# Sixteen steps of a GRU recurrence written as one loop on PE, with one buffer for the state's fp16 parts

## What is computed

```python
def cell(h, x):
    gi = x @ W_ih + b_ih
    gh = h @ W_hh + b_hh
    i_r, i_z, i_n = jnp.split(gi, 3, axis=-1)
    h_r, h_z, h_n = jnp.split(gh, 3, axis=-1)
    r = jax.nn.sigmoid(i_r + h_r)
    z = jax.nn.sigmoid(i_z + h_z)
    n = jnp.tanh(i_n + r * h_n)
    h_new = (1.0 - z) * n + z * h
    return (h_new, h_new)
xs = jnp.swapaxes(inputs, 0, 1)
_, hs = jax.lax.scan(cell, initial_state, xs)
return jnp.swapaxes(hs, 0, 1)
```

## Time and profile before

| | us |
|---|---|
| median of three runs | 2298.03 |
| the three runs | 2296.30 to 2299.89 |
| the profiled execution | 2292.36 |
| span of the profiled execution | 2290.5 |
| PE busy | 2179.2 (95%) |
| DVE busy | 1528.3 (67%) |
| ACT busy | 1279.5 (56%) |

### The profile page before, as it was taken

How to read it: one execution, slowest core, us unless ns; L and a number is a source line. 1 busy time by engine, 2 the same in 40 slices (tenths; PEclk the granted TensorE clock), 3 DMA queues, 4 the chain that set the end, 5 groups by cost and what they waited for, 6 DMA issues and landing times.

```text
span 2290.5 us, 130384 instructions
## 1 busy us (share of the span) xinstructions
PE 2179.2 (95%) x56333; PEld 1837.8 (80%) x56333; DVE 1528.3 (67%) x6093; ACT 1279.5 (56%) x5574; POOL 485.6 (21%) x2271
## 2 busy tenths in 40 slices
PE   5768999999989999999999999999999999999998
PEld 3654655645545899999999999999999999999997
DVE  7987867768677456655665565566666566666665
ACT  6765947749468355566444454454545444454444
POOL 2002121021110122232222222222222222222222
PEclk8569999999999999999999999999999999999999
DMA  5000000010010000000000000000000000000000
GB/s 204 3 2 1 1 1 1 1 56 1 1 56 1 22 4 5 5 5 5 5 5 9 5 9 4 9 10 5 9 9 5 9 5 10 10 5 14 12 9 16
DMA packets 8711, 31.49 MB, mean 14 GB/s; under 512 B 1028, under 2 KB 1352, under 8 KB 7880
## 3 DMA queue, kind: packets, MB, share of 16 engines
q1 hardware_dynamic: 7712, 23.07, 2.7%
q10 hardware_dynamic: 424, 0.07, 0.0%
HBM read 18.94 MB, written 4.19 MB: 10 GB/s over the span
## 4 chain that ended last, share of the span: by engine, by line
PE 82%; DVE 11%; ACT 3%; issue 2%; DMA 1%; POOL 0%; SPq 0%; DVEq 0%; POOLq 0%; ACTq 0%
PE psum L1923 53%; PE psum L1830 9%; PE psum L1733 4%; PE psum L1654 3%; PE psum L1751 3%; PE psum L1696 2%; PE psum L1717 2%; PE psum L1857 2%; DVE region_cols L1102 2%; DVE region_cols L1086 2%; DVE top L1279 1%; PE psum L1673 1%; DMA region_cols<-in_L_cond_W_emb_dram 1%; PE psum L1766 1%; PE psum L1870 1%
## 5 line engine op out<-in xcount | busy, mean ns | idle before, releaser
L563 POOL TENSOR_TENSOR region_w_b<-region_w_b 128x16 f32<-128x16 f32 x1022 | 223.2, 218 | 1153.1 <-DVE region_w_b L1488 1153.1
L1923 PE MATMUL psum<-parts1A,region_w_hh 128*128 128x40 f16 x12288 | 429.6, 179 | 2.9 <-issue 1.1
L1923 PE MATMUL psum<-parts0A,region_w_hh 128*128 128x40 f16 x12288 | 428.9, 179 | 3.1 <-ACT psum L819 0.9
L1923 PE MATMUL psum<-parts1B,region_w_hh 128*128 128x40 f16 x12288 | 428.9, 179 | 1.1 <-issue 0.5
L1923 PE MATMUL psum<-parts0B,region_w_hh 128*128 128x40 f16 x12288 | 428.4, 179 | 1.1 <-issue 0.9
L1923 PEld LDWEIGHTS psum<-parts1A,region_w_hh 128*128 128x128 f16 x12288 | 381.1, 96 | 41.0 <-DVE parts1A L1497 5.7
L1923 PEld LDWEIGHTS psum<-parts0A,region_w_hh 128*128 128x128 f16 x12288 | 380.9, 96 | 40.2 <-DVE parts0A L1497 4.4
L915 ACT ACTIVATE mixA<-rzA 128x8 f32<-128x8 f32 x512 | 110.8, 216 | 535.1 <-DVE rzA L1462 535.1
L1923 PEld LDWEIGHTS psum<-parts1B,region_w_hh 128*128 128x128 f16 x12288 | 363.3, 96 | 3.3 <-issue 1.6
L1923 PEld LDWEIGHTS psum<-parts0B,region_w_hh 128*128 128x128 f16 x12288 | 362.9, 95 | 3.0 <-issue 1.5
L1462 DVE TENSOR_REDUCE rzA<-psum 128x8 f32<-128x32 f32 x512 | 98.2, 192 | 278.9 <-PE psum L1923 278.4
(11 more groups left out here) (243 smaller groups left out, 3303.1 us busy)
## 6 DMA issues: line engine op xcount, KB each, us to landing
region_rows<-in_x_dram SPq DMA_DIRECT2D x4, 1024.0 KB, 11.2
region_w_a<-in_L_cond_W_qkv_dram SPq DMA_DIRECT2D x1, 3072.0 KB, 23.2
region_w_hh<-in_L_cond_W_hh_dram SPq DMA_DIRECT2D x4, 768.0 KB, 6.6
region_w_a<-in_L_cond_W_ih_dram SPq DMA_DIRECT2D x1, 3072.0 KB, 10.2
out_dram<-region_w_b SPq DMA_DIRECT2D x12, 256.0 KB, 2.3
region_cond<-in_cond_dram SPq DMA_DIRECT2D x2, 1024.0 KB, 7.8
region_cols<-in_L_cond_W_emb_dram SPq DMA_DIRECT2D x1, 2048.0 KB, 19.7
region_w_out<-in_L_cond_W_out_dram SPq DMA_DIRECT2D x1, 1024.0 KB, 21.5
```

What stands on the lines that cost most here:

```text
L563: e.tensor_tensor(k.line[half][:, :, :, 1:3], new.unsqueeze(3).broadcast_to([P, 2, B, 2]), k.signs.unsqueeze(1).unsqueeze(1).broadcast_to( ...
L1923: made = e.matmul(k.slots(bank)[:, :, ch, :, 0:2], k.w16[:, 2 * read + c, part, NC * "rzn".index(g) + 2 * half + ch], k.parts[now][read][: ...
```

## The change

Steps 112 to 127 on PE become a loop (`Fori`) of 16 turns over one written-out step, which starts at an instruction address that is a multiple of 256. Waits that count steps (lowA, lowB, putA, putB) are made against a register there. For one body to serve odd and even steps, the parts have one buffer for each half, in all 512 steps. So DVE may write parts A only when PE has read the last step's: unit ABn, the last that reads half A, counts up a new semaphore readA, and `dve_parts` waits for it. For half B nothing is added. The waits of PE on zsumA, nlineA, zsumB and nlineB are left out in all steps. `DVE_STEP` goes from 14 to 15, which moves DVE's cuts (63 instead of 58).

```diff
-DVE_STEP = 14
+DVE_STEP = 15
...
-        self.parts = [[small(f"parts{parity}{half}", 2, B, 2, dtype=FP16) for half in "AB"] for parity in range(2)]
+        self.parts = [small(f"parts{half}", 2, B, 2, dtype=FP16) for half in "AB"]
...
-def dve_parts(e, k, half, st, nxt):
+def dve_parts(e, k, st, half):
     s = k.sem
     h = "AB"[half]
     spread = k.spread[half].rearrange("p c b q -> p (c b) q")
     e.wait_ge(s[f"line{h}"], st + 1)
-    e.tensor_tensor(k.parts[nxt][half][:].rearrange("p c b q -> p (c b) q"), spread[:, :, STATE_AT:HIGH_AT + 1:HIGH_AT - STATE_AT],
+    if half == 0:
+        e.wait_ge(s["readA"], st + 1)
+    e.tensor_tensor(k.parts[half][:].rearrange("p c b q -> p (c b) q"), spread[:, :, STATE_AT:HIGH_AT + 1:HIGH_AT - STATE_AT],
                     spread[:, :, HIGH_AT:NONE_AT + 1:NONE_AT - HIGH_AT], ALU.subtract).then_inc(s[f"low{h}"], 1)
...
+LOOP = (112, 128)
...
-    for st in range(S):
+    for st in range(LOOP[0]):
+        pe_step(e, k, st)
+        pe_side(e, k, st)
+    e.addr_align(256, max_nops=4)
+    with e.Fori(LOOP[0], LOOP[1]) as st:
+        pe_step(e, k, st, st)
+    for st in range(LOOP[1], S):
+        pe_step(e, k, st)
+        pe_side(e, k, st)
...
+def pe_step(e, k, st, turn=None):
+    s = k.sem
+    for u in GRU_UNITS:
...
+        if u in ("AAr", "BAr"):
+            if turn is None and st == 0:
+                e.wait_ge(s["gru_first"], 18)
+                e.wait_ge(s["w_kept"], NC)
+                e.wait_ge(s["w_low"], NC)
             else:
-                pe_row_products(e, k, *args, products, number)
+                e.wait_ge(s[f"low{u[0]}"], st)
+        if u in ("AAr", "ABr"):
+            e.wait_ge(s[f"put{h}"], st + 1)
...
+        if LAST_OF[g, h] == u:
+            made.then_inc(s[f"{g}_products{h}"], 1)
+        elif u == "ABn":
+            made.then_inc(s["readA"], 1)
```

More of the change, by code:

```diff
@@ L82 @@
 r_productsA z_productsA n_productsA r_productsB z_productsB n_productsB
-rsumA zsumA nlineA rsigA giveA tanhA lineA lowA keptA putA
+rsumA zsumA nlineA rsigA giveA tanhA lineA lowA keptA readA putA
 rsumB zsumB nlineB rsigB giveB tanhB lineB lowB keptB putB
@@ L1426, in dve_gru @@
         first = k.state[:, 0, 2 * half:2 * half + 2]
-        e.tensor_copy(k.parts[0][half][:, :, :, 1], first).then_inc(done, 1)
+        e.tensor_copy(k.parts[half][:, :, :, 1], first).then_inc(done, 1)
         e.tensor_copy(k.line[half][:, :, :, 2], first).then_inc(done, 1)
@@ L1430, in dve_gru @@
         e.wait_ge(done, 11 + 4 * half)
-        e.tensor_tensor(k.parts[0][half][:, :, :, 0], first, k.parts[0][half][:, :, :, 1], ALU.subtract).then_inc(done, 1)
+        e.tensor_tensor(k.parts[half][:, :, :, 0], first, k.parts[half][:, :, :, 1], ALU.subtract).then_inc(done, 1)
     e.addr_align(DVE_BLOCK, max_nops=4)
     for st in range(S):
-        nxt = (st + 1) % 2
         dve_r_sum(e, k, st, 0)
@@ L1442, in dve_gru @@
         if st + 1 < S:
-            dve_parts(e, k, 0, st, nxt)
+            dve_parts(e, k, st, 0)
         dve_n_line(e, k, st, 1)
@@ L1446, in dve_gru @@
         if st + 1 < S:
-            dve_parts(e, k, 1, st, nxt)
+            dve_parts(e, k, st, 1)
         if st in PLACE_STEPS:
@@ L1893, in pe_gru @@
         pe_gate_products(e, k, 0, j, range(NC), j)
-    at = {u: i for i, u in enumerate(GRU_UNITS)}
-    final_unit = {(h, g): max((r + h + g for r in "AB"), key=at.get) for h in "AB" for g in "rzn"}
-    for st in range(S):
[L1897 to L1929, removed]
-                pe_gate_products(e, k, *args, products, number)
-            elif kind == "late":
-                pe_late_products(e, k, *args, products, number)
-            elif kind == "next":
-                pe_next_products(e, k, *args, products, number)
-            else:
-                pe_row_products(e, k, *args, products, number)
@@ L1939, in build, with pe_side @@
+def pe_side(e, k, st):
+    for (kind, *args), number, products in SIDE.get(st, ()):
+        if kind == "gates":
+            pe_gate_products(e, k, *args, products, number)
+        elif kind == "late":
+            pe_late_products(e, k, *args, products, number)
+        elif kind == "next":
+            pe_next_products(e, k, *args, products, number)
+        else:
+            pe_row_products(e, k, *args, products, number)
 def build(nc, *args):
```

10 lines of the change are left out of this document (added).

## The result

| | before | after |
|---|---|---|
| median of 20 runs each, the same chip | 2295.24 us | 2300.34 us |
| lowest to highest | 2291.04 to 2300.52 | 2297.26 to 2305.45 |
| profiled execution: span | 2290.5 us | 2297.6 us |
| TensorE steps 111 to 128, start to start | 51.73 us | 55.10 us |

The ratio is 1.0023, with a 95% interval of 1.0015 to 1.0031: the kernel became **5.1 us slower** (3.4 to 7.1), which is about the size that a measurement can tell from no change. The forecast was +2.7 us (2300.7 us), and the time lies inside the range. That it is within 0.4 us of the forecast is luck: the 2.7 were added to a median of three runs (2298.03), the median of twenty is 2.8 us lower, and the difference came out 2.4 us larger. The likeliest case was a change of less than 4.6 us; the centre of the measurement lies just beyond that bound.

A forecast was written before the change was run, and what follows sets the result against it. The prediction took PE as the bound in steps with side product and half B's loop through DVE and ACT in steps 112 to 127. 3.3 - 0.6 + 0 + 0 = +2.7 us gave 2300.7 us, range 2296.0 to 2305.5.

The forecast's parts named there:

- Where the loop's block stands: Ahead of step 112: a block begins 8 instructions before it, so the alignment jumps over the other 248.
- The entry wait: Before step 112: PE waits once, 3.2 to 3.3 us, for the block jumped to; 3.3 us taken.
- Stalls that go: Steps 112 to 128: the loop's 15 further turns fetch nothing, so 0.6 us of fetch stalls go.
- The turn itself: Loop turns: register waits and branch cost 0 to 1.8 us for 16 turns; 0 taken, by half A's room.
- half A's 0.13 us of room: Steps without side product: PE would be ready for half B at 1124.41 but stands still until 1124.55.
- The one buffer, the waits taken out and DVE's cuts: All 511 steps: the readA wait, removed PE waits and 63 DVE cuts stay hidden; 0 us.
- The block is fetched again each turn: Loop's branch back: 15 turns each pay about 2.8 us, 42 us in all, 2343 us; chance 0.10.
- register waits cost more than the room: Loop turns: every 0.1 us beyond half A's room costs 1.6 us; at 0.2 a turn 2303.9 us; chance 0.17.
- the jump finds its block: Loop entry: no wait there, or the loop's fetches were never late; -0.6 us, 2297.4 us; chance 0.14.
- The fetch that the jump might start anew: Loop entry: the jump starts a fetch anew, doubling the entry wait to a sum of +6 us; chance 0.06.
- The change relieves fetching elsewhere: Recurrence: half of 6.4 us of issue waits go and entry costs nothing, -3.8 us, 2294.2 us; chance 0.06.
- Only one block is ahead: PE's code fetch: the next block's packet starts only when the block before it already runs.

The follow-up runs named there:

- experiment 3: The kernel before with only the alignment to 256 ahead of step 112, two buffers and no loop: 2285.63 us, ratio 1.0017 to before.
- experiment 6: The changed kernel again, no edit, on another chip, against the kernel before there: 2294.55 us, ratio 1.0013.
- experiment 7: The changed kernel with its aligned loop from step 114 on (14 turns), against the kernel before: 2293.83 us, ratio 1.0008.
- experiment 2: The changed kernel with the loop but without the alignment ahead of it, against the kernel before: 2282.78 us, ratio 1.0003.
- experiment 1: The changed kernel without loop or alignment, all 512 steps written out, against the kernel before: 2282.25 us, ratio 1.0003.
- Experiment 5: The changed kernel with the loop from step 113 on (15 turns), not aligned, against the kernel before: 2291.29 us, ratio 1.0001.
- experiment 4: The changed kernel with the loop from step 113 on (15 turns), alignment kept, against the kernel before: 2284.34 us, ratio 1.0009.
- experiment 8: The kernel before again, no edit, for its profile alone: 2289.72 us, one run.

## Why the prediction was right, and where it was wrong

**Where the loop's block stands**: right. The jump was at slot 8 of its block, and nearly the whole next fetch was still to come.

**The entry wait**, 3.3 us taken: 3.13 us in the first profile, 2.90 in experiment 3, 3.58 in experiment 6. The sum was right for the wrong parts. The packet started 0.65 us after the side product, not the 1.39 of the earlier trace rows (0.50 in experiment 3, 1.44 in experiment 6); it took 1.28 us, not 0.96; and the first load came 1.72 us after it had landed, not 1.4 to 1.5. The last number is firm: 1.7 in experiments 3 and 6 too. It is the 1.4 to 1.5 of the earlier trace rows, after which the jump is done (1.37, 1.51 and 1.35 us after the landing), and then 0.34 us to the first load (0.14 in experiment 3, where no loop is set up ahead of it). The start of the packet was taken over from a program without the jump. In the ten profiles that have none at this place it lies 1.1 to 1.5 us after the side product; with the jump it came at 0.50 and 0.65, so the jump seems to bring it forward, but in experiment 6 it did not, and why stays open. One reading was wrong: in the source DVE's jump stands behind the instruction at 1159.62 of the earlier trace rows (L1401), not ahead of it, so the 0.10 us are no measure of it. Its own record in the trace of before (L1453) is 0.05 us long, so the 0.10 holds as a bound.

**The missed term**: "The jump waits for the next block ... PE waits 3.2 to 3.3 us, once", and the sum went on as if TensorE afterwards ran as before. It did not: the clock fell to 1.2 GHz for 3.4 us and cost 0.78 us (0.55 to 0.9 in experiments 3, 6 and 7). In the recurrence of before PE never had an idle time of this size, so none of the rows shown there priced it. The Trainium skill has the rule (TensorE: Matmul & The Clock Gate, Why this matters for your kernels: no long idle gaps of TensorE between bursts of matmuls, or the clock drops), and it was not weighed, though the idle time forecast falls under it. The page sets the gap longer than the 1.92 us, and in four profiles 1.62 us, behind which it fell here; the measurement decides.

**Stalls that go**, 0.6 taken: 0.46 by experiment 2, against a before that had 0.65 us of them. Right; the rest goes back in the first turn, 0.09 us longer, and in step 128 (see the one buffer below).

**The turn itself**, 0 taken: right, 2.83 us. But the hand-over of lowA did get 0.07 us longer, inside the 0.04 to 0.14 that was forecast, and with parts A 0.02 us later, as forecast, it leaves 0.03 of half A's 0.13 us of room. A hand-over 0.05 us longer would have cost in every turn.

**The one buffer, the waits taken out and DVE's cuts**, 0: right by experiment 1 (1.0003), to within the measurement. In single steps a little shows: in all ten profiles with the new DVE program, experiment 1 included, step 128 takes 3.20 to 3.21 us, and 3.06 and 3.07 in the two profiles of the old one that have no late block there. One of DVE's cuts now stands after step 127, and the r sum behind it starts 0.54 us after L1401 instead of 0.35. So not every cut is hidden like the one in rows 10. That the cut is the cause was not tested by itself. Summed over the shortest take of each of the 511 steps, the new programs need 0.3 us more.

**The rivals**: "The block is fetched again each turn" is excluded by the queue; "register waits cost more than the room" by the pitch; "the jump finds its block" by the entry. The fetch that the jump might start anew didn't come either: one packet on q8 between 1100.5 and 1103. "The change relieves fetching elsewhere" has nothing for it: outside steps 111 to 128 neither pair of profiles of the two kernels got shorter (see below). "Only one block is ahead" is right for fetching; that what is behind would be lost, which I took up after the result, is wrong.

**What stays open.** In the first pair of profiles the sum is -0.5 for stalls, +3.1 for the entry and +0.8 for the clock, 3.4 us in all, and this is what steps 111 to 128 show. The timed difference is 5.1 us (3.4 to 7.1), on another chip 3.0 (0.9 to 5.0). The remaining 1.7 us of the first lie in other steps of the recurrence or in chance, so of the 2.4 us between the forecast and the measured difference, 0.7 are in steps 111 to 128, the clock above all, and 1.7 are something that no run pins down. I worked out how much longer than the shortest such step of any profile each step outside 111 to 128 was: 13.2 us in sum for before and 17.6 for after. But for the two programs on the next chip it was 9.7 and 17.8, and on the first experiments' chip 2.6 for experiment 1, which has the same DVE program and the same buffer, and 4.3 for experiment 3, which has neither. The steps that are longer lie at other places in each profile. Experiment 5, which has all of the change but the alignment and one of the turns, shows 11.3 us beside the 9.7 of its chip and takes the time of before (1.0001). Four steps a turn, with no entry wait at all, still came out at 1.0012 (1.0002 to 1.0022), with 14.9 us. So late blocks outside the loop vary by several us between executions and chips; whether the changed kernel has a little more of them on some chips is not settled.

No version beat the kernel before: the loop without its alignment saves 0.46 us in its own steps, and that is below what the timing can tell.

## What to carry to other kernels

Before code is aligned, look at which slot of its block the jump will leave: a jump over most of a block that has only just been begun costs nearly a whole fetch, 3 us here, and a loop that fits gains nothing from it. Where an edit makes TensorE idle for some 2 us or more (behind 1.62 us the clock fell in four profiles of twelve), add the price of the lower clock behind it to the sum. A loop on PE over code already run needs no fitting into one block, but it pays only if its fetches were late before, so first add up the weight loads' waits for issue in just those steps.

## What the runs showed of the hardware

- PE's sequencer fetched one block ahead and kept what it had run: loop bodies over one, two, four and seven blocks fetched none of their code again.
- A block is usable 1.4 to 1.5 us after its packet has landed if PE runs into it (1.2 to 1.6 over all such waits of before), and its first matmul ran 1.69 to 1.75 us after the landing when PE jumped there (five entries: after, and experiments 3, 4, 6 and 7; in 4 the packet landed at about 1100.24 and the load ran at 1101.96, in 7 at 1104.77 and 1106.52). The packet started 1.1 to 1.5 us after the side product at this place where no jump stood there, and 0.50, 0.65 and 1.44 us after it with the jump.
- The granted clock fell to 0.50 1.9 us after PE had gone back to work in the first profile (work from 1104.25, fall at 1106.11), 1.6 us after in experiment 3 (1101.63 and 1103.27), at once in experiments 6 and 7, and lasted 3.41 us each time. Behind 1.62 us of idle time at the end of the recurrence it fell in four profiles of twelve (in that of experiment 8 at 2278.67), behind 0.75 us in experiment 4 it did not.
- PE runs through a block of 256 slots in some 3.75 us (193 slots in 2.83). The next block takes about as long: its packet starts 1.1 to 1.5 us after the block has begun, takes 0.9 to 1.5 us, and 1.2 to 1.6 us more go by until it is usable, 3.2 to 4.6 us in all. This fits blocks that come late at places that change from one execution to the next. What makes them late more often on some chips is not shown; the steps were 2.6 us too long in sum on the fastest chip (experiment 1), 9.7 and 13.2 in the kernel before on two slower ones.
- A wait of the sequencer against a register and a taken branch (0.21 us) cost 0.07 us at the hand-over and nothing in the pace of a turn.
